# Macaron layer on one core: eight of 32 state read-outs per chunk on GpSimd with an accumulating DMA, the second softplus a turn later

## What is computed

```python
x = x + 0.5 * ffn(layernorm(x))          # up, gate: 512 -> 2048; down: 2048 -> 512; ternary weights; silu(up) * gate
x = x + attn(layernorm(x))
x = x + 0.5 * ffn(layernorm(x))

# attn: E = 1024 channels, N = 16 states for each channel
r = resid * rsqrt(mean(resid ** 2) + eps) * norm_w
skip, x_in = r @ W_skip, r @ W_in
x = silu(causal_conv4(x_in) + conv_b)
delta = softplus(x @ W_delta_1 @ W_delta_2 + b_delta_2)
Bm, Cm = x @ W_B, x @ W_C
h[l] = h[l-1] * exp(delta[l] * A) + (delta[l] * x[l]) * Bm[l]     # 1024 x 16 states, along the sequence
y[l] = sum over the 16 states of h[l] * Cm[l]
return resid + ((y + x * W_D) * silu(skip)) @ W_out
```

## Time and profile before

| | us |
|---|---|
| median of 3 runs | 2977.1 (2975.74 to 2978.27) |
| the profiled execution, its own time | 2982.67 |
| its span | 2980.9 |
| PE busy | 2767.5 (93%) |
| DVE busy | 2610.2 (88%) |
| POOL busy | 2130.1 (71%) |
| ACT busy | 1845.2 (62%) |

### The profile page before, as it was taken

One profiled execution on the slowest core, in us unless ns is written; L12 is line 12 of the kernel. 1 busy time (PEld: TensorE's weight loads), 2 busy tenths in 40 slices (PEclk: granted clock), 3 DMA queues, 4 the chain that ended last, 5 costly groups with the idle time before them and its releaser, 6 DMA issues.

```text
span 2980.9 us, 53240 instructions
## 1 busy us (share of the span) xinstructions
PE 2767.5 (93%) x18567; PEld 2173.4 (73%) x18567; DVE 2610.2 (88%) x3461; ACT 1845.2 (62%) x4302; POOL 2130.1 (71%) x1983
## 2 busy tenths in 40 slices
PE   4787899999999999999999999999999999999878
PEld 4566677777877777787777778777777877777655
DVE  6378998999989899998989999898999999999992
ACT  6275667575666757566675756667575665767541
POOL 1276777877777787777778777777877777777761
PEclk8898899999999999999999999999999999999898
DMA  7010101001010100101010010101001010101000
GB/s 257 29 36 19 33 19 40 19 26 36 19 40 19 40 19 27 35 19 40 19 40 19 25 37 19 40 18 40 19 25 38 19 40 19 40 19 32 22 29 8
DMA packets 53312, 99.85 MB, mean 33 GB/s; under 512 B 7804, under 2 KB 9144, under 8 KB 52536
## 3 DMA queue, kind: packets, MB, share of 16 engines
q1 hardware_dynamic: 53048, 96.45, 9.8%
HBM read 87.78 MB, written 8.65 MB: 32 GB/s over the span
## 4 chain that ended last, share of the span: by engine, by line
PE 63%; DVE 19%; ACT 8%; issue 8%; POOL 1%; DMA 0%; DVEq 0%; SPq 0%; ACTq 0%; POOLq 0%
PE ps L1552 17%; PE ps L1563 14%; PE ps L1514 10%; PE ps L1575 8%; PE ps L1624 7%; DVE h L1291 7%; DVE y L1317 4%; DVE xc L1361 3%; PE ps L1585 3%; ACT ps L964 2%; PE ps L1605 2%; DVE act L1325 2%; PE ps L1536 1%; DVE xc L1370 1%; ACT xn L909 1%
## 5 line engine op out<-in xcount | busy, mean ns | idle before, releaser
L695 POOL TENSOR_TENSOR h<-u,bb 128x1024 f32<-128x1024 f32 x512 | 1222.4, 2387 | 275.4 <-PE ps L1514 199.8
L1291 DVE TENSOR_TENSOR_SCAN h<-ps,h 128x512 f32<-128x512 f32 x1024 | 1192.2, 1207 | 16.6 <-ACT ps L964 13.7
L964 ACT ACTIVATE ps<-delta,a_neg 128x255 f32<-128x255 f32 x2048 | 881.6, 471 | 447.5 <-DVE h L1291 444.0
L1317 DVE SCALAR_TENSOR_TENSOR y<-ps,ccur,y 128x512 f32<-128x512 f32 x960 | 672.4, 743 | 29.3 <-PE ps L1514 26.9
L1514 PE MATMUL ps<-ident,h 128*128 128x128 f32 x4096 | 558.9, 278 | 95.5 <-DVE y L1317 87.8
L1514 PEld LDWEIGHTS ps<-ident,h 128*128 128x128 f32 x4096 | 471.9, 142 | 178.3 <-issue 94.5
L1552 PE MATMUL ps<-xh,q_up 128*128 128x256 f16 x2048 | 467.6, 275 | 13.1 <-DVE xl L1230 10.1
L1552 PE MATMUL ps<-xl,q_up 128*128 128x256 f16 x2048 | 467.8, 275 | 0.0
L1552 PE MATMUL ps<-xh,q_gate 128*128 128x256 f16 x2048 | 463.5, 273 | 0.0
L1552 PE MATMUL ps<-xl,q_gate 128*128 128x256 f16 x2048 | 463.2, 273 | 0.0
L1563 PE MATMUL ps<-q_down,hh 128*128 128x512 fp8e4 x1024 | 389.1, 380 | 4.6 <-issue 2.8
(11 more groups left out here) (145 smaller groups left out, 3495.8 us busy)
## 6 DMA issues: line engine op xcount, KB each, us to landing
bb<-b_scratch SPq DMA_DIRECT2D x224, 256.0 KB, 3.1
xs<-in_L_attn_resid_dram SPq DMA_DIRECT2D x17, 512.0 KB, 3.6
out_dram<-xs SPq DMA_DIRECT2D x16, 512.0 KB, 4.1
wraw<-in_L_ffn_W_up_dram SPq DMA_DIRECT2D x4, 1024.0 KB, 9.7
wraw<-in_L_ffn_W_gate_dram SPq DMA_DIRECT2D x4, 1024.0 KB, 12.2
wraw<-in_L_ffn_W_down_dram SPq DMA_DIRECT2D x4, 1024.0 KB, 14.2
w_in<-in_L_attn_W_in_dram SPq DMA_DIRECT2D x1, 2048.0 KB, 21.3
w_skip<-in_L_attn_W_skip_dram SPq DMA_DIRECT2D x1, 2048.0 KB, 9.1
```

Of the source, the lines that this page charges most:

```text
L695: pl.tensor_tensor(h[:, s % RING, :, :], u[:, :, :], bb[:, planes_of(s) % 2, s % PLANES:s % PLANES + 1, :].broadcast_to([P, HE, CH]), ALU. ...
L964: ins = ac.activation(abar[r][:, e, 1:], delta[:, k, 1:], ACT.Exp, scale=a_neg[:, k, n:n + 1])
L1291: v.tensor_tensor_scan(hr, abar[r].rearrange("p e t -> p (e t)"), hr, 0.0, ALU.mult, ALU.add).then_inc(scanned, 1)
L1317: ins = v.scalar_tensor_tensor(out=yy, in0=hT[:, t, :], scalar=cc, in1=yy, op0=ALU.mult, op1=ALU.add)
```

## The change

Six things are changed.

1. **Read-out on POOL.** For the steps in `ELEM` (8 of the 32 of a chunk; 10 in the first, 8 in the last) PE does no transposes and DVE no `y_add`. POOL multiplies `h` by a row of C spread over the partitions (`state_times_c`, 128 x 1024, into the single buffer `hc`) and then, from its own queue, starts a DMA of 512 KB that adds `hc` to the half of `xw` (`accum_op=ALU.add`). The product waits for the scan of its step, for its C row and for the DMA before it (`elem_added`); `y_plus_x` waits for all such DMAs of its half.
2. **C by DMA.** B and C are transposed together (32 rows for 16), C goes to a DRAM scratch of its own, and SP loads one row for each such step into one of four buffers (`load_c`, 128 KB).
3. **x*D on ACT**, as 8 activations of 128 x 256 a turn, in slots 3 and 11 as before.
4. **First residual sum on ACT.** x + layernorm(x) = x * (1/sigma + 1) - mean/sigma is one activation for each of the two tiles, in place; POOL adds 1 to the row of factors. Normalisation "p" and POOL's addition go.
5. **Softplus by halves.** `D2_2` and `D2_3` move to the next turn (slots 3 and 4), and the second half's Exp and Ln follow there; `ln1` and `relu1` are gone, both halves use `tmp`.
6. **All gate products on DVE** (`POOL_PAIRS` and `gate_copy` go), and new slot tables.

The diff, cut to its core (of the tables only the first rows of the loop's):

```diff
-    ["T1_0", "T1_1", ("OM_0", 0, 4), "U1_0"],
-    ["G1_0", "U1_1"],
-    ["G1_1", "U1_2"],
-    ["G1_2", "U1_3"],
-    ["G1_3", "YT_2"],
...
+    ["T1_0", "T1_1", ("OM_0", 0, 4)],
+    ["U1_0", "G1_0", "U1_1", "G1_1"],
+    ["U1_2"],
+    ["G1_2", "D2_2", "U1_3"],
+    ["G1_3", "D2_3", "YT_2"],
...
-POOL_PAIRS = {1: [6], 2: [4]}
-GATES = 2
 XD_0 = 3
 XD_1 = 11
 NEXT_LN_FILL = 19
 NEXT_LN = 29
-MASK_1 = 8
-MASK_0 = 27
+MASK_1 = 6
+MASK_0 = 28
 MASK_H = 1
-SP_1 = 4
-EDGE_STEPS, RSTD_STEPS, RMS_STEPS = 5, 5, 10
+ELEM = [3, 8, 11, 15, 17, 22, 27, 31]
+ELEM_FIRST = [4, 7, 11, 13, 15, 19, 21, 22, 27, 31]
+ELEM_LAST = [3, 6, 8, 10, 15, 23, 27, 30]
+ELEM_PLANES = 4
+ELEM_AHEAD = 6
+EDGE_STEPS, RSTD_STEPS, RMS_STEPS = 5, 5, 11
 
...
+def loads_of_c(c, q):
+
+    last = [max(s for s in range(STEPS) if planes_of(s) == k - 2) for k in range(2, LOADS)]
+    at = {s: min((k for k in range(2, LOADS) if last[k - 2] >= s - ELEM_AHEAD), default=LOADS) for s in elem_of(c)}
+    return [s for s in elem_of(c) if at[s] == q]
+
...
-        ln1 = sb("ln1", [P, HE, CH])
-        relu1 = sb("relu1", [P, HE, CH])
-        gates = relu1[:, :, :].rearrange("p (g e) t -> p g (e t)", g=GATES)
+        hc = sb("hc", [P, HE, CH])
+        cplane = sb("cplane", [P, ELEM_PLANES, CH])
...
-                sp.dma_start(b_dram, bT[:, :]).then_inc(b_stored, 16)
+                sp.dma_start(b_dram, bT[0:N, :]).then_inc(b_stored, 16)
+                g = elems_before(c, 0)
+                for k in range(ELEM_PLANES):
+                    need(sp, c_loaded[k], 16 * ((g - 1 - k) // ELEM_PLANES + 1))
+                    sp.sem_inc(sp_go, 1)
+                sp.dma_start(c_dram, bT[N:2 * N, :]).then_inc(c_stored, 16)
                 sp.wait_ge(b_stored, 16 * (c + 1))
                 sp.sem_inc(sp_go, 1)
...
+            def load_c(c, s):
+
+                g, n = elems_before(c, s), state_of(s)
+                need(sp, times_c, g - ELEM_PLANES + 1)
+                sp.sem_inc(sp_go, 1)
+                sp.wait_ge(c_stored, 16 * (c + 1))
+                sp.sem_inc(sp_go, 1)
+                sp.dma_start(cplane[:, g % ELEM_PLANES, :], c_dram[n:n + 1, :].rearrange("o t -> (o t)").partition_broadcast(P)
+                             ).then_inc(c_loaded[g % ELEM_PLANES], 16)
 
...
-                need(pool, hT_ready, 2 * used + 2)
+                if S >= RING and not is_elem(used // STEPS, used % STEPS):
+                    need(pool, hT_ready, 2 * rows_before(used // STEPS, used % STEPS) + 2)
+                elif S >= RING:
+                    need(pool, times_c, elems_before(used // STEPS, used % STEPS) + 1)
...
+            def state_times_c(i, s):
+
+                S, half, g = STEPS * i + s, s // N, elems_before(i, s)
+                k = g % ELEM_PLANES
+                need(pool, c_loaded[k], 16 * (g // ELEM_PLANES + 1))
+                need(pool, scanned, 2 * S + 2)
+                need(pool, elem_added, 16 * g)
+                go()
+                pl.tensor_tensor(hc[:, :, :], h[:, s % RING, :, :], cplane[:, k:k + 1, :].broadcast_to([P, HE, CH]),
+                                 ALU.mult).then_inc(times_c, 1)
+                need(pool, xw_ready, 2 * i + half + 1)
+                need(pool, times_c, g + 1)
+                pool.dma_start(xw[:, half * HE:(half + 1) * HE, :], hc[:, :, :], accum_op=ALU.add).then_inc(elem_added, 16)
...
+                pl.tensor_tensor(rt[:, 0, :], rt[:, 1, :], ones[:, 0:TB], ALU.add).then_inc(rms_step, 1)
...
-            def x12(ph, i):
-
-                k = i + 1
-                need(pool, xn_ready, TB * ln_run(ph, i, "p") + TB)
-                need(pool, xr_ready, k + 1)
-                go()
-                slot = k % XSLOTS
-                pl.tensor_tensor(xs[:, slot, :, :], xs[:, slot, :, :], xn[:, :, :], ALU.add).then_inc(x12_ready, 1)
-
             def softplus(c, half):
 
-                need(pool, sp_step, 4 * (c + 1))
+                need(pool, sp_step, 4 * c + 2 * half + 2)
                 dd = delta[:, half * HE:(half + 1) * HE, :]
-                if half == 0:
-                    pl.tensor_tensor(dd, dd, tmp_h, ALU.add).then_inc(delta_ready, 1)
-                else:
-                    need(pool, abar_ready, 2 * STEPS * c)
-                    go()
-                    pl.tensor_tensor(dd, relu1[:, :, :], ln1[:, :, :], ALU.add).then_inc(delta_ready, 1)
+                pl.tensor_tensor(dd, dd, tmp_h, ALU.add).then_inc(delta_ready, 1)
...
+                    step = step_of(ph, i, s)
+                    if step and is_elem(*step):
+                        state_times_c(*step)
...
+            def x_times_d(i, half):
+
+                need(sc, z_ready, 4 * i - 2 + 2 * half)
+                need(sc, xc_ready, 2 * i + 2)
+                for b in range(half * HE, (half + 1) * HE):
+                    ins = ac.activation(xw[:, b, :], xc[:, b, :], ACT.Copy, scale=wd[:, b:b + 1])
+                ins.then_inc(xw_ready, 1)
...
-                mag = tmp_h if half == 0 else ln1[:, :, :]
+            def softplus_log(ph, i, c, half):
+
                 for q in (2 * half, 2 * half + 1):
-                    bk, before = job_no("fill", -1, f"D2_{q}")
-                    need(sc, bank_used[bk], before + 1)
-                ac.activation(mag, mag, ACT.Exp, scale=-1.0).then_inc(sp_step, 1)
-                need(sc, sp_step, 2 * half + 1)
-                ac.activation(mag, mag, ACT.Ln, bias=1.0).then_inc(sp_step, 1)
-
-            def softplus_log(ph, i):
-
-                c = i + 1
-                for q in range(QT):
                     bk, before = job_no(ph, i, f"D2_{q}")
                     need(sc, bank_used[bk], before + 1)
...
+            def x12(ph, i, slot):
+
+                need(sc, xr_ready, i + 2)
+                for t in range(TB):
+                    ins = ac.activation(xs[:, slot, t, :], xs[:, slot, t, :], ACT.Identity, scale=rt[:, 0, t:t + 1],
+                                        bias=rt[:, 7, t:t + 1])
+                ins.then_inc(x12_ready, 1)
...
+                    if after(ph, "D2_3", 1, s):
+                        softplus_log(ph, i, i, 1)
+                    if after(ph, "D2_3", 2, s):
...
+                if is_elem(i, s):
+                    return
...
-                need(ve, xw_ready, 2 * (i if q < 2 else i - 1) + q // 2 + 1)
+                c = i if q < 2 else i - 1
+                need(ve, xw_ready, 2 * c + q // 2 + 1)
+                need(ve, elem_added, 16 * elems_before(c, N * (q // 2 + 1)))
...
-                    if step:
+                    if step and not is_elem(*step):
```

More of the change, by code:

```diff
@@ L158 @@
     ["DB"],
[L159 to L160 removed]
+    ["DT", "D2_0"],
+    ["D2_1"],
     [],
@@ L355, in ffn_run @@
     return 2 * i + (kind - 1) if ph == "loop" else (2 * NCH - 2 if ph == "last" else 2 * NCH - 1)
-def gate_no(ph, i, kind, p):
-    done = {"fill": (0, 0), "first": (1, 0), "loop": (i + kind, i - 1), "last": (NCH, NCH - 2), "drain": (NCH, NCH - 1)}[ph]
-    return sum(len(POOL_PAIRS[k]) * n for k, n in zip((1, 2), done)) + POOL_PAIRS[kind].index(p)
 def ln_run(ph, i, kind):
@@ L1020, in conv_in @@
                 if far_on_pool(ph, q // 2):
-                    if q < 2:
-                        need(sc, x12_ready, i + 2)
-                    else:
-                        need(sc, delta_ready, 2 * i + 2)
+                    if q < 2 and "T2_0" in PHASES[ph]:
+                        for k in range(2):
+                            t2, before = job_no(ph, i, f"T2_{k}")
+                            need(sc, bank_ready[t2], before + 1)
                     for e in range(2):
```

281 lines of the change are left out of this document (133 added, 148 removed), and 23 rows, old and new, of the table LOOP_SLOTS.

## The result

| | before | after |
|---|---|---|
| median of 4 runs, us | 2977.7 (2975.7 to 2978.5) | 2941.7 (2937.0 to 2945.3) |
| ratio | | 0.9878 (0.9865 to 0.9890) |
| the profiled execution, own time | 2982.7 | 2940.3 |
| its span | 2980.9 | 2938.7 |

The change makes the kernel 36 us faster (1.2%). The forecast was 100 us, 2877; the range (2825 to 2960) holds the time. Most of its terms can be found in the trace, but 64 of its 100 us aren't there, and the wait that costs most lies at a place for which it charged nothing.

The account below looks back on a forecast made before the run. PE sets the pace for some two thirds of a loop turn, DVE for one third. A turn gains 8.6 - 3.4 + 1.0 = 6.2 us, 87 over 14; first turn 7, tail 6: together 100, 2877 us, range 2825 to 2960.

Parts of the forecast that it names:

- the landing: Time for an adding DMA's 512 KB to arrive in xw: 6.65 us, the middle between 3.6 and 9.7.
- Not all of it counts ... I take half: DVE's addition of YT_0 to xw waits 6.8 us for step 15's DMA; half, 3.4 us a turn, was charged.
- the gain of 9.6 us a turn (8.6 + 1.0): Per loop turn: 8.6 us from dropped read-outs and transposes, 1.0 from ACT's lighter block at the turn's end.
- this cover: POOL's 41 us of idle time a turn and its waits for PE's transposes; its added work was charged nothing directly.
- DVE's third: The third of a loop turn at DVE's pace; read-outs of steps 11, 15 and 17 there were worth 4.2 us.
- the first turn: It drops ten read-outs, worth at most 14 us and at least nothing; 7 us of gain was taken.
- the tail: It drops eight read-outs, worth at most 11 us; 6 us of gain was taken, with the start of the drain.
- POOL becomes the bound: Rival: DMA issues of 2.39 us put POOL at 162.5 us of a 171.5 us turn; 2937 us, chance 0.12.
- The landing is hidden: Rival: the DMA lands in 3.6 us or less, turns of 164.4 to 166.3 us; 2830 with whole gain, chance 0.14.
- The landing holds DVE up: Rival: at YT_0 the wait is landing minus 2.6 plus 2.8 us; about 3069 at 16 us landing, chance 0.13.
- Collisions: Rival: DVE's two L1370 instructions a turn and POOL's SBUF reads block each other, 3.4 us a turn; 2925, chance 0.03.

Follow-up runs that it names:

- adds_aside: The changed kernel with its adding DMAs issued as before but into a DRAM scratch, DVE not waiting for them (a time probe, y incomplete): 2874.7 us.
- no_adds: The changed kernel without the adding DMAs and all waits for them, POOL's products kept (a time probe, y incomplete): 2862.1 us.
- six: The changed kernel with steps 15 and 31 given back to PE and DVE, six steps a loop turn on POOL: 2957.1 us.
- four: The changed kernel with only steps 8, 15, 22 and 31 of a loop turn on POOL, still by DMA: 3020.0 us.
- before_twice: The kernel before the change, with POOL computing u times B twice at the eight steps a turn: 3050.1 us.

## Where the prediction held, and why it was wrong in size

**Right.** The direction and the range. PE's work in a loop turn: forecast 162.2, measured 161.2. The product: 2.4, measured 2.36. An adding DMA on POOL's queue: 1.35 taken between 0.32 and 2.39, measured about 1.45 with its wait. POOL in a turn: 154.2, measured 150.6 and 4.4 of waits for its own products. ACT's second pair of table loads isn't among the costly lines of the chain; no run tests it. The Trainium skill ("DMA: Bandwidth & Descriptors", Anatomy of one DMA) led to an estimate of 3.2 us for the landing, the prediction took 6.65; the trace has 4.5 at the median, and the measurement decides:
```profile
xw<-hc POOLq DMA_DIRECT2D x130, 512.0 KB, 4.5
```

**Wrong, first step: the place and the share of the landing ("Not all of it counts ... I take half").** The sum charged 3.4 us a turn at `YT_0`, half of a wait of 6.8, and nothing at `YT_2`: 48 over the loop. The landing was shorter than taken, the wait at `YT_0` is 1.8 us on average, and `YT_2` waits 2.0 where nothing was expected; the sum of 3.8 lies near the forecast's 4 to 7 by luck. It is `YT_2` whose landing the chain goes through, once in each of the 14 loop turns. It was let off because there is a whole slot more between DMA and use; but the DMA's start isn't set by its slot, it stands behind POOL's back-to-back stretch at the turn's border (1343.5 to 1363.0). And the wait counts in full: in the loop turns of the profiled executions adds_aside takes 2337.3 us and the kernel after 2401.8, 64.5, where 48 was charged. 17 us of the miss are here.

**Wrong, second step: the gain of 9.6 us a turn (8.6 + 1.0).** With the landing out of the chain the prediction would have had 14 x 9.6 = 134 us less in the loop; adds_aside has 2425.2 - 2337.3 = 88, or 6.3 a turn. 46 us of the miss are here, the larger part. It isn't POOL's issues, since a turn without them (no_adds) has 6.7. What the runs show of the 2.9 us a turn that are then still missing is this.

DVE fell by 4.1 us in the turn shown, to 155.7, and not by 10.5 to 149.3. Contention of its two-SBUF instructions gives 3.9 of the missing 6.4 (62 us over 16 chunks). Most of the rest is the price of a read-out: 743 ns is its mean duration, but in busy time six and four pay 0.64 us for each that they give back to DVE, once the contention is taken out, since the rows overlap.

Contention was priced in the prediction (3.4 us a turn, 48 in all, a chance of 0.03). Its expectation was for `xc<-tmp,xc`, and there it stands in the chain: in 13 of the 14 loop turns of no_adds the chain has one of them at about 3 us, where one undisturbed takes 1.23.
```profile
1253.81 2.98 DVE xc L1372
```
In the kernel before the chain has two pieces of that line in most turns, 0.59 and 1.35. So contention can be some 1 to 1.7 us of the 2.9; this is an estimate from rows, as no run takes it away. Of the mask's share 6 to 10 us of time in all are shown.

And POOL was charged nothing, because 41 us of idle time seemed to cover 21. before_twice shows that this cover was never whole: 18.7 us more of POOL cost 4 us a turn even in the kernel before. At that rate of 0.2 the products and what they replace (+10.4 us) would take 2 of the 2.9 us; that is an estimate from another kernel, and it holds some contention too. How the 46 us divide between POOL's load, contention and an overrated gain in "DVE's third" stays open.

**Wrong in small:** the first turn was to gain 7 and gained 0; the tail was to gain 6 and gained 12, with 7 more ahead of the first turn. Together 13 forecast and 19 measured.

**The rivals.** "POOL becomes the bound" named 2937 and a turn of 171.5, and 2941.7 and 171.6 (the mean of the loop's intervals) were measured; but it got there with issues of 2.39 us and POOL at 162.5, and neither came. Its number was right by luck, since most of what held the turn up was the landing. "The landing is hidden" fell: it is not hidden at 4.5 us. "The landing holds DVE up" had the right mechanism but only the place at `YT_0`: by its formula a landing of 4.5 makes a wait of 4.7 there, and 1.8 was measured. "Collisions" was given 0.03; 62 us of DVE's time and the row above say that it deserved more.

## What to carry over

A DMA within a chain costs the wait for its source and the landing, here 0.55 and 4.5 us from the issue, and all of that stood in front of DVE. Let the DMAs add what is needed late, and let an engine add the last one: a pass of 2.4 us saved 37 us here. Idle time of an engine is cover only where it lies: before giving an engine work, load it artificially in the old kernel (before_twice took one small edit) and read the price. And when DVE's instructions with two operands in SBUF, even the smallest, get a new place beside POOL's passes, look at how long each takes.
